# Selector products from transposed sums in place of triangle products, in the middle block of a three-block kernel

## The reference, cut to what matters

```python
dt = softplus(dt + dt_bias)                    # per token and head, 8 heads
A = -exp(A_log);  dA = exp(dt * A)
dBx = dt[..., None, None] * x_ssm[..., None] * Bmat[:, :, None, None, :]
def step(s, inp):                              # the scan over the tokens
    s = s * dA_t[..., None, None] + dBx_t
    y = einsum('bhpn,bn->bhp', s, C_t)
```

## Time and profile before

| | us |
|---|---|
| median of 3 runs | 1349.55 |
| lowest and highest | 1346.49, 1356.04 |
| the profiled execution, its own time | 1361.64 |
| its span from first to last instruction | 1359.9 |
| PE busy, DVE busy in that span | 1093.3, 819.1 |
| ACT busy, POOL busy | 608.5, 685.0 |

### The profile page before, as it was taken

One profiled execution on the slowest core, in us unless ns is written; L12 is line 12 of the kernel. 1 busy time (PEld: TensorE's weight loads), 2 busy tenths in 40 slices (PEclk: granted clock), 3 DMA queues, 4 the chain that ended last, 5 costly groups with the idle time before them and its releaser, 6 DMA issues. The chain is left out here.

```text
span 1359.9 us, 22804 instructions
## 1 busy us (share of the span) xinstructions
PE 1093.3 (80%) x6900; PEld 908.5 (67%) x6900; DVE 819.1 (60%) x1626; ACT 608.5 (45%) x1438; POOL 685.0 (50%) x607
## 2 busy tenths in 40 slices
PE   3737999999816889998999999989627999999900
PEld 3736999999704666676667676666526999999800
DVE  6984444444348889778979777764374444444433
ACT  2313555555415555555555555545313555555400
POOL 6945555555312555556545545556335555555300
PEclk9999999999957899879988889999756999999955
DMA  7851222222132011111111100000061222222187
GB/s 239 256 247 51 78 77 76 79 76 77 51 114 70 24 35 42 41 37 40 40 44 38 37 24 16 17 16 24 28 247 44 78 79 76 78 78 75 55 270 228
DMA packets 73247, 112.27 MB, mean 83 GB/s; under 512 B 10664, under 2 KB 60336, under 8 KB 71856
## 3 DMA queue, kind: packets, MB, share of 16 engines
q1 hardware_dynamic: 47888, 58.77, 12.8%
q0 software_dynamic: 13824, 37.77, 8.7%
q10 hardware_dynamic: 11424, 14.30, 3.2%
HBM read 66.76 MB, written 44.04 MB: 81 GB/s over the span
## 5 line engine op out<-in xcount | busy, mean ns | idle before, releaser
L401 POOL DMA_INDIRECT ys_d<-xs,row_of x144 | 142.4, 989 | 193.8 <-DVE xs L765 187.4
L754 DVE TENSOR_TENSOR xl<-pT,xh 128x256 fp32r<-128x256 f32 x144 | 61.2, 425 | 218.2 <-PE pH L570 118.5
L459 ACT ACTIVATE hs<-pH 128x512 f32<-128x512 f32 x144 | 86.2, 598 | 233.1 <-PE pH L570 227.9
L396 POOL DMA_INDIRECT xs<-xn_d,token_of x144 | 140.1, 973 | 52.2 <-issue 42.7
L759 DVE TENSOR_TENSOR h2l<-hs,h2h 128x512 fp32r<-128x512 f32 x144 | 99.8, 693 | 77.8 <-ACT h2h L467 76.7
L1524 DVE SCALAR_TENSOR_TENSOR acc<-raw,cwh,acc 128x512 f32<-128x512 f32 x104 | 120.0, 1201 | 2.9 <-POOL acc L1056 1.9
L590 PE MATMUL pY<-w2h,h2h 128*128 x576 | 103.3, 301 | 0.4 <-DVE h2l L759 0.3
L570 PE MATMUL pH<-w1h,xh 128*128 x288 | 92.8, 404 | 1.8 <-DVE xl L754 1.0
L570 PE MATMUL pH<-w1l,xh 128*128 x288 | 92.8, 404 | 0.0
L590 PE MATMUL pY<-w2h,h2l 128*128 x576 | 92.2, 282 | 0.0
L1041 POOL TENSOR_TENSOR yv<-yv,sz 128x512 f32<-128x512 f32 x32 | 44.9, 1404 | 92.9 <-DVE yv L1574 92.9
(11 more groups left out here) (240 smaller groups left out, 2714.6 us busy)
## 6 DMA issues: line engine op xcount, KB each, us to landing
m_yg<-ys_d SPq DMA_DIRECT2D x64, 128.0 KB, 2.1
xs<-ys_d SPq DMA_DIRECT2D x16, 512.0 KB, 6.1
wst<-in_L_ffn_w_dram ACTq DMA_DIRECT2D x8, 512.0 KB, 4.5
xs<-in_L_attn_x_dram SPq DMA_DIRECT2D x8, 512.0 KB, 5.9
hs<-in_L_ffn_w_dram ACTq DMA_DIRECT2D x8, 512.0 KB, 4.7
xn_d<-xs SPq DMA_DIRECT2D x8, 512.0 KB, 3.2
lo_d<-w1l SPq DMA_DIRECT2D x1, 4096.0 KB, 11.1
lo_d<-w2l SPq DMA_DIRECT2D x1, 4096.0 KB, 21.3
```

The source lines that it names most:

```text
L396: pool.indirect_dma_start(out=xg[:, t % NX, :], out_offset=None, in_=xn_d, in_offset=bass.IndirectOffsetOnAxis(ap=token_of[:, t:t + 1], ax ...
L401: pool.indirect_dma_start(out=ys_d, out_offset=bass.IndirectOffsetOnAxis(ap=row_of[:, t:t + 1], axis=0), in_=y[:, t % NX, :], in_offset=No ...
L459: act.activation(r[:, u, :], pH[u][:, :], ACT.Relu).then_inc(relu_done.sem, 1)
```

## The change: what it does

- `sum_up`'s group now has a third small f32 product in kind 3, `pCumT`: DA as the stationary operand against the triangle. Its output has the 32 pairs of chunk and head on partitions and the 128 tokens along the row, so it is the cumulative sum, transposed.
- It is split into three bf16 parts that are stacked on 96 partitions of `cumT`: the first part by ACT straight from PSUM (between L1173 and L1174 of before), the rest by DVE subtractions and a cast inside `sum_up`, and two ACT copies that move them to partitions 32 to 63 and 64 to 95. ACT waits there for a new semaphore, rest_done. `al_done` now comes from ACT in kind 0, where before it came from DVE in kind 3.
- `sums` makes one product a head: the stationary operand is one column of `pick` broadcast to [96, 128], which has a one at the three partitions of that pair, and the moving operand is `cumT`. For a chunk that is 8 products in place of 24. The mask products stay.
- `al`, `tri_bf` and the five DVE operations of the split are gone. POOL makes `pick` with a memset and three selects ahead of its other constants; PE and DVE wait for 6 links of that chain where they waited for 3.

```diff
+        CH = GC * H
+        pick = sb("pick", [3 * CH, CH], BF16)
+        cumT, rest, mid = sb("cumT", [3 * CH, 2, P], BF16), sb("m_rest", [CH, 2, P]), sb("m_mid", [CH, P], BF16)
-        al = sb("al", [P, 3, 3, GC * H], BF16)
+        pCumT = small[0:CH, 320:320 + P]
...
-            chain.link(pool.memset(raw[:, :, 0:CONV - 1], 0.0))
+            pool.memset(raw[:, :, 0:CONV - 1], 0.0)
+            chain.link(pool.memset(pick[:, :], 0.0))
+            for part in range(3):
+                chain.link(pool.affine_select(out=pick[:, :], in_=pick[:, :], compare_op=ALU.not_equal, fill=1.0,
+                                              base=-part * CH, pattern=[[-1, CH]], channel_multiplier=1))
...
                 if G is not None:
                     act.wait_ge(cum_ready.sem, cum_ready.done(G))
                     act.activation(row(G, ECUM), pCum, ACT.Exp)
+                    act.activation(cumT[0:CH, G % 2, :], pCumT, ACT.Copy)
                     act.activation(row(G, ETOT), pTot, ACT.Exp).then_inc(exps.sem, 1)
...
                     act.activation(row(G, DEC), row(G, DEC), ACT.Exp).then_inc(dec_out.sem, 1)
+                    act.wait_ge(rest_done.sem, rest_done.done(G))
+                    act.activation(cumT[CH:2 * CH, G % 2, :], mid[:, :], ACT.Copy)
+                    act.activation(cumT[2 * CH:3 * CH, G % 2, :], rest[:, 1, :], ACT.Copy).then_inc(al_done.sem, 1)
...
-            pe.wait_ge(consts, 3)
+            pe.wait_ge(consts, 6)
...
-                    for part in range(3):
-                        pe.matmul(pE[:, n * P:(n + 1) * P], al[:, G % 3, part, col:col + 1].to_broadcast([P, P]), tri_bf[:, :],
-                                  start=(n == 0 and part == 0), stop=False, skip_group_check=True)
+                    pe.matmul(pE[:, n * P:(n + 1) * P], pick[:, col:col + 1].to_broadcast([3 * CH, P]), cumT[:, G % 2, :],
+                              start=(n == 0), stop=False, skip_group_check=True)
...
                     pe.matmul(pCum, tri[:, :], row(G, DA), start=True, stop=True)
+                    pe.matmul(pCumT, row(G, DA), tri[:, :], start=True, stop=True)
...
-                link(dve.tensor_copy(tri_bf[:, :], tri[:, :]))
...
-                dve.wait_ge(a_done.sem, a_done.done(G))
-
-                linked(dve.tensor_copy(al[:, G % 3, 0, :], row(G, DA)))
-                linked(dve.tensor_tensor(row(G, DS), row(G, DA), al[:, G % 3, 0, :], ALU.subtract))
-                linked(dve.tensor_copy(al[:, G % 3, 1, :], row(G, DS)))
-                linked(dve.tensor_tensor(row(G, DS2), row(G, DS), al[:, G % 3, 1, :], ALU.subtract))
-                dve.tensor_copy(al[:, G % 3, 2, :], row(G, DS2)).then_inc(al_done.sem, 1)
...
                 dve.wait_ge(cum_copied.sem, cum_copied.done(G))
+                linked(dve.tensor_tensor(rest[:, 0, :], pCumT, cumT[0:CH, G % 2, :], ALU.subtract))
                 dve.tensor_tensor(row(G, DEC), pTot, row(G, NCUM), ALU.add).then_inc(dec_in.sem, 1)
+                dve.wait_ge(al_done.sem, al_done.done(G - 1))
+                linked(dve.tensor_copy(mid[:, :], rest[:, 0, :]))
+                dve.tensor_tensor(rest[:, 1, :], rest[:, 0, :], mid[:, :], ALU.subtract).then_inc(rest_done.sem, 1)
```

More of the change, by code:

```diff
@@ L851, in mamba_block @@
         negA, bias = sb("negA", [P, GC, H]), sb("m_bias", [P, GC, H])
-        ident_bf, tri_bf = sb("ident_bf", [P, P], BF16), sb("tri_bf", [P, P], BF16)
-        future = sb("future", [P, GC, P], BF16)
+        CH = GC * H
+        ident_bf, future = sb("ident_bf", [P, P], BF16), sb("future", [P, GC, P], BF16)
+        pick = sb("pick", [3 * CH, CH], BF16)
+        cumT, rest, mid = sb("cumT", [3 * CH, 2, P], BF16), sb("m_rest", [CH, 2, P]), sb("m_mid", [CH, P], BF16)
         xr = sb("xr", [P, RX, D])
@@ L898, in mamba_block @@
             step(n) for n in ("xT", "xT_hi", "xT_lo", "z", "tz", "sz", "dt", "dt_added", "x2T", "x2T_copied", "logit", "logit_copied"))
-        soft, exp_u, a_done, al_done, cum_ready, cum_copied, exps, dec_in, dec_out, decdt, halo = (
-            step(n) for n in ("soft", "exp_u", "a", "al", "cum", "cum_copied", "exps", "dec_in", "dec_out", "decdt", "halo"))
+        soft, exp_u, a_done, al_done, rest_done, cum_ready, cum_copied, exps, dec_in, dec_out, decdt, halo = (
+            step(n) for n in ("soft", "exp_u", "a", "al", "rest", "cum", "cum_copied", "exps", "dec_in", "dec_out", "decdt", "halo"))
         p_ready, raw_done, tap0, tap_act, tap1, taps, tb_done, xc_done = (
@@ L1073, in _ @@
         def _(act):
-            for s in (norm_done, norm2_done, x2T_copied, logit_copied, xT_hi, tz_done, exp_u, exps, dec_out, raw_done, tap0, tap_act, tb_done,
+            for s in (al_done, norm_done, norm2_done, x2T_copied, logit_copied, xT_hi, tz_done, exp_u, exps, dec_out, raw_done, tap0, tap_act, tb_done,
                       xt_done, bt_done, ex0_done, ex_done, sq_done, yT_copied):
@@ L1379, in _ @@
         def _(dve):
-            for s in (add1, add2, stats, aggr, stats2, aggr2, var_done, nmr_done, xT_lo, sz_done, dt_added, soft, a_done, al_done, cum_copied, decdt, dec_in, halo,
+            for s in (add1, add2, stats, aggr, stats2, aggr2, var_done, nmr_done, xT_lo, sz_done, dt_added, soft, a_done, rest_done, cum_copied, decdt, dec_in, halo,
                       taps, xc_done, M_done, S_done, t1_done, t2_done, xo_done):
@@ L1390, in split_weights @@
                 dve.wait_ge(loads, 7 * 16)
-                dve.wait_ge(consts, 3)
+                dve.wait_ge(consts, 6)
                 for n in range(KI):
@@ L1463, in split_x @@
                 dve.tensor_tensor(xTl[:, q, :, tok(i)], by_head(pXN, KD), xTh[:, q, :, tok(i)].bitcast(F32), ALU.subtract).then_inc(xT_lo.sem, 1)
-            NCH = 2 + 5 + (len(ATANH) - 1) + 2 + 4
             chained = [0]
```

## The result

The changed kernel is slower: 1381.99 us (median of 4 runs, 1372.09 to 1388.91) against 1350.78 us (4 runs), a ratio of 1.0218 with a 95% interval of 1.0172 to 1.0264. I had forecast 1337 and a range up to 1354. The profiled execution, at 1372.09 us, is the shortest of the four, so its rows show the mildest form of what happened; the profiled execution of the kernel before, 1361.64 us, is longer than the median of its runs, so the two profiles stand only 10.5 us apart where the medians stand 31 apart.

What follows compares the result with a forecast made beforehand. PE was taken to set 15 of 32 slots, DVE mostly the others; -13.5 - 6.6 + 4.8 + 3.2 = -12.1 us from the median of 1349.55 gave 1337 us, range 1320 to 1354.

Steps and rivals of the forecast that it cites:

- What bounds the kernel: Mamba block: PE sets kind 1 and the last slots, DVE kinds 0 and 2; PE sets any slot with fallen clock.
- the 15 slots that PE sets: Of 32: eight of kind 1, four more at the end, three at low clock; elsewhere a removed product lengthens a wait.
- Rival C: Kind 0: thinner PE work brings more low-clock stretches, 4.5 to 7.2 us each; five more give 1367 us; chance 0.10.
- The products' term: Sums: 16 fewer products a chunk at 56 ns, 0.90 us in each of 15 chunks, 13.5 us less.
- The split's term: Kind 3: DVE's five split operations go, 1.1 us in each of six slots, 6.6 us less.
- sum_up and pCumT: DVE's new operations in kind 0 add 4.8 us; the transposed product and ACT's copy delay from_state, adding 3.2 us.
- Hidden work: Kind 0's later dec_in, ACT's wait and two copies, and POOL's start-up constants were taken to cost nothing.
- Rival D: Hand-over in kind 0: the hidden work is uncovered, 2.3 + 7.7 = 10 us, giving 1347.4 us; chance 0.05.

Runs made afterwards that it cites:

- e7: The changed kernel plus unneeded PE products in two waits of kind 0 only (four and five products); 1369.17 us, ratio 1.012.
- e4: The changed kernel plus unneeded PE products in its waits, nine in kind 0 and five in kind 2; 1353.42 us, ratio 1.0015.
- e2: The kernel before with only the first bf16 part in the sums, so 8 triangle products a chunk; 1373.71 us, ratio 1.0194.
- e9: The changed kernel plus unneeded PE products in all the larger waits of PE's loop; 1345.1 us, ratio 0.996.
- e10: The kernel before plus the same unneeded PE products in all the larger waits as e9; 1341.46 us, ratio 0.9929.
- e3: The changed kernel with DVE's split of the transposed sums and ACT's two copies moved from kind 0 to kind 1; 1380.51 us, ratio 1.0223.
- e11: The changed kernel with the split moved to kind 1 as in e3, plus the full fill of unneeded PE products as in e9; 1355.64 us, ratio 1.0007.
- e1: The changed kernel with three selector products a head, one for each part, so 24 a chunk again; 1374.92 us, ratio 1.0198.

## Why the prediction was wrong

*What bounds the kernel.* Which engine sets which kind of slot was right at full clock. What I made of it was not: I counted PE's products only in the 15 slots that PE sets, and took a longer wait of PE in the others as free. Rival C, which I had at one in ten, is what came.

*The step that failed* is the argument against rival C: "PE gets sparser mostly in slots where it has spare time, and there a fallen clock costs little." The fall does begin in such a slot, but it doesn't end there. It is paid in the next one, which PE sets: kind 1 behind kind 0, 18.30 and 22.20 us against 16.90, and in e7 kind 3 behind kind 2. I gave C one chance in ten, and asked for five stretches as long as those of the earlier trace rows; the block's half-clock time rose from 507.40 x 0.18 = 91 us to 514.20 x 0.24 = 123 us in the mildest of the runs. The timed runs say how much of the loss this is. The whole program's mean granted clock is 0.869 to 0.882 in the four runs of the changed kernel, median 0.874, and 0.892 to 0.907 in 25 of the kernel before, median 0.899. That is some 75 us more at the lower level, and within the runs of either kernel one such microsecond goes with 0.34 to 0.41 us of time: an estimate of 26 to 31 us, nearly all of the 31. That e4 takes 28 us off with added work, and e2 adds 20 with work removed, shows it.

*The products' term*, -13.5 us. The price of a product, 56 ns, was right, and in the last four slots the term came in full (12.40 to 11.5). In kind 1 it was 0.5 of 0.9 us at a held clock. Kind 1 is then no longer PE's alone (PE busy 14.26 of 16.20 in e4); at full clock PE waits 0.83 us there for POOL's `yv`, as in the kernel before, and 0.89 us for ACT's `ex`, which is new.

*The split's term*, -6.6 us. DVE's five operations went, but kind 3 at full clock fell by 0.3 to 0.4 us, not 1.1; pCumT's 0.34 us are in it, since a slot is counted from from_state and pCumT stands ahead of that. "PE loses 0.9 us in the same slots and so doesn't become the bound at once" was too hopeful: PE is busy 14.87 of 15.60 there.

*sum_up and pCumT*, +4.8 and +3.2 us. In kind 0 I had 1.2 us; e9 against e10 show 1.1. The sum was right for the usual groups. Its parts lie otherwise: the product's 0.34 us belong to kind 3, and all of kind 0's goes when DVE's split moves away, for in e3's order (e11) kind 0 is at 16.0 us. So that cost is one of place.

*Hidden work.* The start-up took what it took before: the first chunk begins at 455.50 against 455.30. Rival D, the wait for ACT's copies, didn't come. A hand-over cost of another sort did, once: PE's 3.48 us for POOL's long product in the last group's kind 0, where I had written that PE hides the work. The forecast has no term for it.

*At a held clock* the terms as measured are 7 x (1.1 - 0.5 - 0.1), -0.9 x 4 for the last slots unfilled, and 4 for the last group's kind 0: about 4 us more instead of 12 less. The rest, some 27 of the 31 us, I put to the clock, by the estimate above. What is not shown is why the clock, once fallen, stays low so much longer in the changed kernel.

## What to carry to other kernels

Where the granted clock moves within a stage, ask of a product taken away not only whether PE sets this slot, but whether the wait that it leaves grows and what PE has to do right behind it. Try the reverse before the saving: unneeded products in the waits of a kernel tell in one run what its clock costs, and here they made the untouched kernel 1.1% faster. Fill every wait or look at all kinds of slot afterwards, since the fall may move to another place, as in e7.

## What the runs showed of the hardware that I had not expected

The clock fell from its upper level, 2.4 GHz, to the lower, 1.2 GHz, at waits of 1.50 and 1.79 us that began 2.1 us apart, with only a group of five bf16 products between them, and stayed there for 10.2 to 17.0 us. In the kernel before, with waits of at most 0.97 and 1.35 us at the same two places, it fell as well, but for 3.5 us. e1 has waits of 1.06 and 1.34 us there and long falls, so the two waits don't tell the whole. A microsecond at the lower level went with 0.34 to 0.41 us of time within the runs of one kernel. Between the unfilled and the filled block it was about 0.23 us, the fill's own cost taken off: 514.20 - 488.50 us for 123 - 10 us in the changed kernel, 507.40 - 487.20 for 91 in the one before. Products whose results nobody reads held the clock up too: with nine of them in kind 0 and five in kind 2 (e4), three of the five kind 1 slots that had been at 0.65 to 0.81 ran at 1.00. And a product of POOL that took 1.27 us in the kernel before took 5.63 beside six of DVE's taps in the changed one.
